# A four-stage sequence model on one core: who writes the attention mask, where the D skip and three small steps stand

## What is computed

```python
# Mamba block, x0 = rmsnorm(x), 256 inner channels, 16 states
s = s * exp(d * A) + (d * u) * B          # one scan per state, over the tokens
y = sum_n(s * C)  +  u * D_skip           # per token
y = y * silu(z);  x = x + y @ out_proj    # then RMS norm
x = x + fc3(relu(fc2(relu(fc1(rmsnorm(x))))))

# one attention layer, 8 heads of 64, windows of 64 tokens
sim = q @ k.T                              # own window and the one before
sim = where(mask, -big, sim)               # later keys, keys over 64 back, no window before the first
x = x + softmax(sim) @ v @ wo
h = (h - mean) / sqrt(var + 1e-5)          # of the shifted rows
a, g = split(h @ w1 + b1);  x = x + (a * gelu(g)) @ w2 + b2
```

## Time and profile before

| | us |
|---|---|
| median of 3 runs | 1754.76 (1754.00 to 1755.98) |
| the profiled execution | 1752.11 |
| its span | 1750.3 |
| TensorE busy | 1421.7 (81%) |
| VectorE busy | 1239.9 (71%) |
| ScalarE busy | 1039.4 (59%) |
| GpSimd busy | 931.7 (53%) |

### The profile page before, as it was taken

How to read it: one execution, slowest core, us unless ns; L and a number is a source line. 1 busy time by engine, 2 the same in 40 slices (tenths; PEclk the granted TensorE clock), 3 DMA queues, 4 the chain that set the end, 5 groups by cost and what they waited for, 6 DMA issues and landing times. The chain is left out here.

```text
span 1750.3 us, 24605 instructions
## 1 busy us (share of the span) xinstructions
PE 1421.7 (81%) x8356; PEld 760.5 (43%) x8356; DVE 1239.9 (71%) x1774; ACT 1039.4 (59%) x1794; POOL 931.7 (53%) x484
## 2 busy tenths in 40 slices
PE   6747099767667888888788768999999999999988
PEld 2215088622222333333333335555555555555553
DVE  2965043238699899989998198777777777777763
ACT  4423045268766565666665256777777777777754
POOL 0430723300598788787877066655555555555541
PEclk9866599888799999999999789999999999999999
DMA  1006211210000000003000011111111111111110
GB/s 61 0 6 137 72 48 48 71 46 1 3 0 1 1 1 0 1 1 126 1 1 1 14 43 33 42 37 31 35 33 31 37 26 38 33 46 31 37 25 25
DMA packets 48850, 53.57 MB, mean 31 GB/s; under 512 B 10420, under 2 KB 32102, under 8 KB 48359
## 3 DMA queue, kind: packets, MB, share of 16 engines
q1 hardware_dynamic: 46438, 47.46, 10.9%
q0 software_dynamic: 2304, 4.74, 0.8%
HBM read 19.63 MB, written 9.47 MB: 17 GB/s over the span
## 5 line engine op out<-in xcount | busy, mean ns | idle before, releaser
L1147 POOL TENSOR_TENSOR ssm_dbu<-ssm_dtu,ssm_b_all 128x1024 f32<-128x1024 f32 x128 | 302.0, 2376 | 49.1 <-ACT ssm_b_all L1071 48.4
L1766 POOL TENSOR_TENSOR at_direct<-at_direct,home_dt 128x1024 f32<-128x1024 f32 x64 | 152.4, 2381 | 323.0 <-DVE home_dt L1856 323.0
L930 PE MATMUL ssm_bank<-ssm_seen,ident 128*128 128x512 f32 x512 | 254.0, 620 | 35.4 <-POOL ssm_seen L1156 28.1
L1065 ACT ACTIVATE ssm_bank<-home_dt,ssm_decay 128x512 f32<-128x512 f32 x256 | 173.8, 690 | 98.0 <-DVE ssm_state L1254 97.0
L1254 DVE TENSOR_TENSOR_SCAN ssm_state<-ssm_bank,ssm_dbu 128x512 f32<-128x512 f32 x128 | 148.7, 1207 | 17.0 <-POOL ssm_dbu L1147 11.9
L1254 DVE TENSOR_TENSOR_SCAN ssm_state<-ssm_bank,ssm_carry,ssm_dbu 128x512 f32<-128x512 f32 x128 | 156.3, 1267 | 5.7 <-ACT ssm_bank L1065 4.4
L930 PEld LDWEIGHTS ssm_bank<-ssm_seen,ident 128*128 128x128 f32 x512 | 96.7, 194 | 123.4 <-issue 75.0
L1559 PE MATMUL at_two<-home_u,at_hs 128*128 128x512 f32 x256 | 129.1, 628 | 8.9 <-ACT at_kT L1703 4.8
L1891 DVE TENSOR_REDUCE at_peak<-at_scores 128x8 f32<-128x1024 f32 x64 | 78.4, 1225 | 78.2 <-PE at_scores L1619 65.4
L1771 POOL TENSOR_TENSOR home_u<-home_u,at_inv 128x1024 f32<-128x1024 f32 x64 | 121.5, 1899 | 20.7 <-DVE at_inv L1867 20.7
L1777 POOL TENSOR_TENSOR at_direct<-at_direct,at_rnorm 128x1024 f32<-128x1024 f32 x64 | 123.2, 1924 | 0.2
(11 more groups left out here) (239 smaller groups left out, 3366.5 us busy)
## 6 DMA issues: line engine op xcount, KB each, us to landing
at_v_mix<-at_v SPq DMA_DIRECT2D x112, 128.0 KB, 2.3
at_hs<-branch SPq DMA_DIRECT2D x64, 128.0 KB, 2.3
moe_w<-in_moe_w SPq DMA_DIRECT2D x16, 256.0 KB
moe_to_experts<-moe_empty SPq DMA_DIRECT2D x10, 258.0 KB, 7.2
moe_slot_rows<-moe_to_experts SPq DMA_DIRECT2D x10, 258.0 KB, 2.9
x<-in_x SPq DMA_DIRECT2D x8, 256.0 KB, 3.7
moe_rows<-moe_from_experts SPq DMA_DIRECT2D x8, 256.0 KB, 4.9
home_dt<-in_turn SPq DMA_DIRECT2D x2, 1024.0 KB
```

Of the source, the lines that this page charges most:

```text
L930: last = nc.tensor.matmul(bank[Y0 + half][:], ident[:], seen[:, n % 2, half], start=n == 0, stop=False)
L1065: nc.scalar.activation(bank[DA0 + half][:], chunk_of(dt[:, half], t), ACT.Exp, scale=decay[:, half, n:n + 1]).then_inc(r[f"da{half}"], 1)
L1147: nc.gpsimd.tensor_tensor(dbu[:, i % RING], dtu[:, t % 2], b_all[:, i % 2:i % 2 + 1, :].broadcast_to([P, 2, CH]), ALU.mult).then_inc(r["db ...
L1766: nc.gpsimd.tensor_tensor(direct[:, n % TURNED], direct[:, n % TURNED], crossed[:, n % 2], ALU.add).then_inc(s["added"], 1)
```

## The change

Five edits:

- The mask. For every tile but the first, ScalarE copies the mask (bf16, repeated over the heads) into `scores`, behind its exponential and ahead of its logarithm; a semaphore `masked` tells TensorE, whose products then add to it. The two mask products with the identity remain for tile 0 alone.
- Centring and the third values' product swap places: `centring` goes from the head of phase 3 to the tail of phase 2 (step 1), `values(..., (2,))` from the tail of phase 2 to the head of phase 3 (step 6). ScalarE's square of the centred rows and VectorE's third `prods` go with them.
- The D skip opens a chunk's sum: its two products stand ahead of the chunk's first, behind the wait for the gate of the chunk before.
- The root of the RMS norm is written to PSUM bank `W1`, and VectorE reads it there.
- The x add, the centring, its square, the variance, its root and `ready` all come one index later; `LAST_STEP` grows by one.

```diff
@@ mamba, TensorE
+                    if n == 0:
+                        for half in range(2):
+                            nc.tensor.matmul(bank[Y0 + half][:], skip_w[:, half], chunk_of(u[:, half], t),
+                                             start=True, stop=False)
                     for half in range(2):
                         last = nc.tensor.matmul(bank[Y0 + half][:], ident[:], seen[:, n % 2, half],
-                                                start=n == 0, stop=False)
-                    if n == STATES - 1:
-                        for half in range(2):
-                            last = nc.tensor.matmul(bank[Y0 + half][:], skip_w[:, half], chunk_of(u[:, half], t),
-                                                    start=False, stop=True)
+                                                start=False, stop=n == STATES - 1)
@@ mamba, the later steps: TensorE centring 12 -> 13, variance 14 -> 15; ScalarE 13 -> 14, 15 -> 16
-                t = posted(i, 12)
+                t = posted(i, 13)
...
@@ mamba, ScalarE
-                nc.scalar.activation(at, at, ACT.Exp, scale=-0.5).then_inc(rooted, 1)
+                nc.scalar.activation(at if to is None else to, at, ACT.Exp, scale=-0.5).then_inc(rooted, 1)
...
-                    log_and_root(t, W1, r["logged"], r["rstd"])
+                    log_and_root(t, W1, bank[W1][:], r["logged"], r["rstd"])
@@ mamba, VectorE
-                    nc.vector.tensor_tensor(chunk_of(dt[:, 0], t), chunk_of(branch, t), chunk_of(dt[:, 1], t), ALU.mult
+                    nc.vector.tensor_tensor(chunk_of(dt[:, 0], t), chunk_of(branch, t), bank[W1][:], ALU.mult
-                t = posted(i, 9)
+                t = posted(i, 10)
                     dve.wait_ge(r["down"], up_to(t))
...
-                t = posted(i, 14)
+                t = posted(i, 15)
                     dve.wait_ge(r["rooted"], up_to(t))
@@ ffn, TensorE
-                if chunk_at(g, 2) is not None:
-                    centring(chunk_at(g, 2))
+                if chunk_at(g, 6) is not None:
+                    values(chunk_at(g, 6), (2,))
...
-                if chunk_at(g, 5) is not None:
-                    values(chunk_at(g, 5), (2,))
+                if chunk_at(g, 1) is not None:
+                    centring(chunk_at(g, 1))
...
+                    opening = opens(n)
                     if n == 0:
                         pe.wait_ge(s["masks"], 32)
-                    opening = int(opens(n))
-                    for parity in range(2):
-                        nc.tensor.matmul(scores[:, parity].rearrange("p (h j) -> p h j", h=4), eye16[:],
...
+                    else:
+                        pe.wait_ge(s["masked"], n)
@@ ffn, ScalarE
+                n = g - SCORE
+                if real(n) and n >= 1:
...
+                    act.wait_ge(s["shifted"], up_to(n - 1))
+                    opening = int(opens(n))
+                    nc.scalar.activation(scores[:].rearrange("p a (h j) -> p (a h) j", h=4),
+                                         mask[:, opening:opening + 1].broadcast_to([P, HEADS, TILE]), ACT.Copy
+                                         ).then_inc(s["masked"], 1)
...
-                c = chunk_at(g, 2)
+                c = chunk_at(g, 1)
@@ ffn, VectorE
-                    prods(chunk_at(g, 5), range(PARTS_OF_HID))
+                    prods(chunk_at(g, 5), (0, 1))
+                if chunk_at(g, 6) is not None:
+                    prods(chunk_at(g, 6), (2,))
```

More of the change, by code:

```diff
@@ L754 @@
 POST = STATES + 4
-LAST_STEP = POST + (2 * SEQS - 1) * STATES + 15
+LAST_STEP = POST + (2 * SEQS - 1) * STATES + 16
 APART = (3, 7, 11, 15)
@@ L1595, in _ @@
                         pe.wait_ge(s["shifted"], up_to(n - 1))
+                    opening = opens(n)
                     if n == 0:
                         pe.wait_ge(s["masks"], 32)
[L1598 to L1602 removed]
+                        for parity in range(2):
+                            nc.tensor.matmul(scores[:, parity].rearrange("p (h j) -> p h j", h=4), eye16[:],
+                                             mask[:, 1:2].broadcast_to([P, 4, TILE]),
+                                             start=True, stop=False, skip_group_check=True)
+                    else:
+                        pe.wait_ge(s["masked"], n)
                     windows = n % PER_CHUNK * TILE
```

16 lines of the change are left out of this document (8 added, 8 removed).

## The result

The changed kernel takes **1725.4 us** (median of 4 runs, 1724.85 to 1726.97) against 1755.0 for the kernel before in the same session (1754.00 to 1755.98): a ratio of 0.9833, 95% interval 0.9816 to 0.9850, 1.7% faster. The forecast was 1724, with a range of 1716 to 1738. The profiled execution takes 1724.85 us with a span of 1723.1, 27.2 us less than the span before.

What follows compares the result with a forecast made beforehand. VectorE was taken to bound the scan, TensorE the attention stage. The profiled 1752.1 - 11.9 (scan) - 19.1 (attention) = 1721.1; with the median 2.65 us above the profiled run, 1724 us was forecast, range 1716 to 1738.

Steps and rivals of the forecast that it cites:

- x add, -10.3: Scan: one step later, VectorE's seven waits for the MLP's product go, 1.47 us each, counted whole as -10.3 us.
- rival B: Scan gives nothing because GpSimd or the clock takes back the x add's gain; only attention gains: 1736 us, 13%.
- Root, -3.1: Scan: root in PSUM shortens VectorE's product and GpSimd's instruction beside it; only GpSimd's share, 7 x 0.45 us, arrives.
- Skip and `ready`: Scan: wait moves from gate to L1223; +0.5 us at six boundaries, +0.2 at the first, -1.7 at the end.
- phases 0 (0), 2 (-0.45, -1.32) and 3 (-0.29): Attention steps, g modulo 4: us gained in each without mask products, limited by ScalarE's copy of transposed weights before `av`.
- Phase 1 (-0.29): Attention step, g modulo 4 = 1: without masks `av` starts 0.05 us behind the copy, -0.29 us; later gelu costs nothing.
- The account of the mask: Attention: TensorE loses two mask products on 63 tiles and the third values' product's wait; periods 43.2 and 42.3 us.
- A: Attention: TensorE alone sets the pace, ScalarE never late; masks and waits come in full: 1690 us, 3%.
- C: Attention gains a third: gelu late for `wo`, or copies hold each other up, 1 us a period: 1737 us, 6%.
- D: Slower than before: ScalarE's mask write dearer than any row its size; at half read rate 1764 us, 6%.
- E: Scan: the root in PSUM doesn't shorten VectorE's product; 3 us less gain, 1727 us, inside the forecast's range.
- What would show it: Signs: 1.0 us mask writes, 0.9 us copy waits in phases 0 and 2; wrong if clock falls or GpSimd waits grow.

Runs made afterwards that it cites:

- e1: Kernel before with only the x add, the centring behind it, its square, variance, root and `ready` one step later: 1755.6 us, ratio 0.9996.
- e2: Kernel before with only the root of the RMS norm written to PSUM and read there by VectorE: 1752.9 us, ratio 0.9984.
- e3: Kernel before with only the D skip opening a chunk's sum instead of closing it: 1751.3 us, ratio 0.9980.
- e5: Changed kernel with `ready` ahead of L1223 in VectorE's order: 1722.6 us, ratio 0.9806.
- e7: Changed kernel with ScalarE's mask write of phase 1 behind the v copy instead of ahead of the gelus: 1723.7 us, ratio 0.9817.
- e4: Kernel before with only the swap of centring and third values' product, the mask left on TensorE: 1729.9 us, ratio 0.9858.
- e10: Changed kernel with the edits of e5, e7 and e8 together: 1703.4 us, ratio 0.9710.
- e8: Changed kernel with the mask of phase 2 (16 of 64 tiles) back on TensorE as two products: 1718.6 us, ratio 0.9785.
- e12: Changed kernel with each ScalarE mask write done twice, the second when the first has landed: 1774.1 us, ratio 1.0116.
- e9: Kernel before with e1's edit, and TensorE's idle stretch filled by moving the first half of fc2's product earlier: 1739.1 us, ratio 0.9916.

## Why the prediction was right, and where not

**Sum.** 1724 was forecast, 1725.4 measured. Both stages gave less than forecast (10.4 for 11.9, 14.8 for 19.1). That is 5.8 us short. The time came out within 1.4 because the part ahead of the scan was 2.0 us shorter in the profiled execution by scatter, and because the forecast added 2.65 from the profiled time to the median, where it is now 0.5 (the rest is rounding of the forecast). That closeness is luck; without it the forecast would have been some 6 us too low, still inside its range.

**x add, -10.3.** The waits went as said: none inside the scan. That the whole 10.3 arrives can't be confirmed by itself. The changed kernel has one chunk without a low stretch, the first: 58.63 us for 60.15 before, 1.5 less where the terms give 1.7 (1.47 + 0.45 - 0.2). Alone (e1) the step gave the median nothing, and of its 7.5 us the clock took some 3. The step that fails is the sentence "so I count the whole wait as gained": it looked for GpSimd to take the gain back, and the engine that took a part was TensorE by its clock. The forecast had the clock only as +-4 us and in rival B. In the changed kernel this did not come to bear, since the low stretches in the middle of a chunk are three as before.

**Root, -3.1.** Mechanism and size stand: 0.68 us for 1.58, GpSimd's increments 299.2 us busy in all for 302.0 (2.8 less, 3.2 forecast; there were six stretched ones, of 2.80 to 2.82 us, and not seven), -2.8 us in e2's median. By the Trainium skill, "SBUF — State Buffer", "SBUF: two separate sides", VectorE with two SBUF inputs and GpSimd lock each other out for a whole instruction; the trace agrees, since with the root in PSUM GpSimd's instruction beside it takes 2.34 us again instead of 2.80. VectorE's wait for `dbu` grew from 2.8 to 5.7 us; that is most of the part of VectorE's 7 x 0.9 that does not arrive.

**Skip and `ready`.** Right in mechanism and place: 6.86 us from gate to L1223, seven waits of 2.1 to 2.2, e3's boundary at nothing and the scan's end at -1.7 (5.6 for 7.3). e5 bears out that `ready` cost 0.6 us a boundary there. Together the three terms gave -1.42 a chunk; measured are 61.39 - 60.01 = -1.38. Some 0.3 of it is the clock (an estimate): the three late low stretches of before, 2.5 us a pair less 1.7, are gone.

**Attention, phases 0 (0), 2 (-0.45, -1.32) and 3 (-0.29).** Right. From one set of q and k transposes to the next, phase 0 is at 9.57 us for 9.54 in the mean, phase 2 at 10.61 and 10.60 for 11.04 and 11.90 (-0.43, -1.30), phase 3 at 9.46 for 9.74 (-0.28). The steps from copy to copy used above begin and end inside a phase, so each shows a part of two: phase 3's gain is in the step that ends in phase 0.

**Phase 1 (-0.29).** This term is wrong: the phase takes 13.93 and 12.90 us in turn, before 13.90 and 13.03, 0.05 less in the mean. It fails at "No cost, but the margin is under 0.1 us": the gelus, 0.93 us later, held the product with `wo` up by 0.08, and the transposes and the copy with it by 0.15. e7 shows it, with 13.77 and 12.75. The rest of the 0.29 was not there in every period: it was read from phase 3's rows, and in phase 1 of the period of the earlier trace rows, before the change, the copy ends at 1212.60 and `av` starts 0.23 behind it, not 0.34:

```profile
1211.58 1.02 ACT L1754 ACTIVATE home_z<-at_two 128x1024 f32<-128x1024 f32 x1 [2.97 <-PE at_two L1589]
```

```profile
1212.83 0.29 PE L1647 MATMUL at_one<-home_z,at_v 64*64 64x64 f32 x4
```

13 x 0.24 = 3.1 us is most of the 4.3 that the stage lacks. The last tiles gave 2.7 us and the stretch behind the last copy took 2.6, of which 1.7 with the low clock (e4, e7 and e10 take 31.5 there); the forecast had both at nothing.

**The account of the mask.** The periods 43.57 and 42.53 were forecast as 43.2 and 42.3. But the prediction's story, that the change gains by taking the masks from TensorE, is only half true: e4 and e8 show that the swap gives it all and that the mask write takes 0.42 us a period back. The prediction had the pieces, "New are the mask write ahead of all these (+0.93)", and never asked what the swap would give without the mask: 1.65 a period by its own rows, measured 1.58. It was right that a dearer write would be on the path in phases 0 to 2 and hidden in 3 (e12: 1.05, 1.07, 1.05, 0.02).

**The rivals.** A is out: `av` waits 19.4 us for the copy. B is not what happened, but its second cause, the clock, is real: e1 is in part B for one edit. C is half true in its cause, gelu late for `wo`, with 0.16 us a period (e7) and not 1. D is out, at 1.025 us a write. The Trainium skill, "ScalarE: Activation LUTs", "What ACT_TABLE_LOAD costs", charges 93 ns for a per-partition operand; this write has none, and it shows none of the 0.1 us between the forecast's lower and upper price. E is out.

**What would show it.** The waits for the copy came as said in phases 0 and 2, at 1.04 and 0.69 for 0.9. The mask writes, the root's product and the waits at L1223 came as said. Of the signs of being wrong, the granted clock is 0.95 in the scan as before and 0.98 for 0.99 in the attention stage, with the stretch behind the last copy, and VectorE waits for GpSimd 2.9 us more in all.

## What to carry to other kernels

When two edits stand in one change, ask for each what it would give without the other; here an engine freed by the one was not what bounded the phase, and moving work to the engine that did cost a quarter of the gain (0.42 of 1.58 us a period). Put moved work on the engine that has slack in that phase, phase by phase, not for all tiles alike. And a wait that is removed from one engine can be taken back in part by the clock of another: look at the granted clock around TensorE's idle stretches, and fill such a stretch with a product that is ready.

## What the runs showed of the hardware

- TensorE's granted clock fell to 0.50 for 3.4 us at a time, right behind idle stretches of 2.0 to 2.8 us in a stage where it otherwise works 50 of 60 us. One low stretch in the middle of a chunk costs 1.7 us (60.11 for 58.40 in e5 and e10). One some 10 us behind the gate costs little or nothing: in e9 chunks take 58.43 us with it and 58.42 without, and 59.23 either way; the fifth chunk takes 61.15 us in the changed kernel, with one, and 60.92 in e8, without. The idle stretch alone does not decide it: before, at 630.06, TensorE went on at full clock behind 2.15 us idle, and in e5 at 630.36 behind 2.80. What does decide it, and why e5 has one such stretch in the middle of its chunks where the changed kernel has three, stays open. That filling the stretch removes it there is shown (e9: none of six at that place).
- ScalarE writing 128x1024 float32 to PSUM from a 2-byte source repeated eight times takes 1.025 us, as long as its copy of float32 out of PSUM.
